# One adaLN transformer block on one core: out projections by single tiles in every even step, and an ffn product in plain fp32

## The reference

```
h = layernorm(x) * (1 + ca) + sa
x = x + ga * attention(h) @ Wo.T          # 8 heads of 64, keys and values from a latent of 64
h = layernorm(x) * (1 + cb) + sb
x = x + gb * (h @ weight.T + pooled(h) @ disha)
```

## Time and profile before

| | |
|---|---|
| three runs, median (lowest to highest) | 3177.59 us (3172.59 to 3179.52) |
| the profiled execution | 3168.62 us |
| its span, first to last instruction | 3166.8 us |
| mean granted TensorE clock | 0.997 |
| busy: PE / DVE / ACT / POOL | 96% / 71% / 54% / 80% |
| attention slot 8 of 16, step 0 to step 0 | 192.80 us |

### The profile page before, as it was taken

The page is one execution under the profiler, slowest core; times in us unless marked ns, Lnnn a source line. Parts: engine busy times, 40 slices in busy tenths (PEclk is TensorE's granted clock), DMA queues, the critical chain, the costliest instruction groups (busy, mean ns, idle before and its releaser), DMA issues.

```text
span 3166.8 us, 45191 instructions
## 1 busy us (share of the span) xinstructions
PE 3047.3 (96%) x15394; PEld 1679.0 (53%) x15394; DVE 2236.2 (71%) x2484; ACT 1721.5 (54%) x3209; POOL 2549.1 (80%) x1520
## 2 busy tenths in 40 slices
PE   6999999999999999999999999999999999999998
PEld 4445555555555555555555455555555555555445
DVE  5567767776777777777767777776777777776665
ACT  3555555555555555555555555555555555555544
POOL 3878787988878888788887878888787887888787
PEclk9999999999999999999999999999999999999999
DMA  2111111121112111121111211211121111211111
GB/s 83 43 43 51 53 57 44 48 64 45 54 45 68 41 48 58 48 61 45 51 48 51 64 44 48 64 45 51 48 67 42 48 58 48 61 38 45 48 45 47
DMA packets 165348, 162.92 MB, mean 51 GB/s; under 512 B 62208, under 2 KB 113536, under 8 KB 165120
## 3 DMA queue, kind: packets, MB, share of 16 engines
q1 hardware_dynamic: 165120, 160.05, 17.2%
HBM read 74.40 MB, written 17.33 MB: 29 GB/s over the span
## 4 chain that ended last, share of the span: by engine, by line
PE 61%; DVE 16%; POOL 10%; issue 6%; ACT 6%; DMA 1%; SPq 0%; DVEq 0%; POOLq 0%; ACTq 0%
PE ps_mix L628 17%; PE ps_score L649 11%; PE ps_score L651 9%; POOL prob_sum L1021 8%; PE ps_max L677 7%; DVE neg_max L1173 6%; PE ps_side L614 6%; PE ps_side L743 4%; PE ps_side L762 3%; ACT probs L851 2%; DVE query L1215 2%; PE ps_side L729 2%; ACT query L897 2%; DVE mixed_lo L1191 1%; DVE h_lo L1205 1%
## 5 line engine op out<-in xcount | busy, mean ns | idle before, releaser
L1021 POOL TENSOR_TENSOR prob_sum<-prob_sum,probs 128x1024 f32<-128x1024 f32 x768 | 1898.6, 2472 | 329.6 <-ACT probs L851 255.7
L1173 DVE TENSOR_REDUCE neg_max<-ps_max 128x1 f32<-128x1024 f32 x1024 | 1202.9, 1216 | 391.2 <-PE ps_max L677 387.2
L851 ACT ACTIVATE probs<-ps_score 128x512 f32<-128x512 f32 x2048 | 1112.3, 596 | 559.6 <-PE ps_score L651 506.6
L628 PE MATMUL ps_mix<-probs,values 128*64 128x512 f32 x4096 | 937.1, 599 | 0.8 <-ACT probs L851 0.8
L649 PE MATMUL ps_score<-query,key_hi 128*128 128x512 f32 x2048 | 888.9, 434 | 31.6 <-ACT probs L851 25.1
L651 PE MATMUL ps_score<-query_m,key_lo 128*128 128x512 f32 x2048 | 809.5, 395 | 0.0
L628 PEld LDWEIGHTS ps_mix<-probs,values 128*64 128x64 f32 x4096 | 271.7, 137 | 534.1 <-issue 532.9
L649 PEld LDWEIGHTS ps_score<-query,key_hi 128*128 128x128 f32 x2048 | 384.4, 188 | 316.9 <-ACT probs L851 156.1
L1021 POOL TENSOR_TENSOR prob_sum<-probs 128x1024 f32<-128x1024 f32 x128 | 317.4, 2479 | 142.1 <-ACT probs L851 142.1
L651 PEld LDWEIGHTS ps_score<-query_m,key_lo 128*128 128x128 f32 x2048 | 386.7, 189 | 42.5
L677 PE MATMUL ps_max<-key_hi,query 64*128 64x512 f32 x2048 | 375.7, 444 | 27.5 <-DVE neg_max L1173 26.1
(11 more groups left out here) (191 smaller groups left out, 2759.3 us busy)
## 6 DMA issues: line engine op xcount, KB each, us to landing
query_m<-query SPq DMA_DIRECT2D x128, 256.0 KB, 2.4
query_m<-query SPq DMA_DIRECT2D x256, 128.0 KB, 2.4
recip<-recip_scratch SPq DMA_DIRECT2D x254, 128.0 KB, 2.9
x_in<-in_L_attn_x_dram SPq DMA_DIRECT2D x32, 512.0 KB, 4.7
x_mid<-in_L_attn_x_dram SPq DMA_DIRECT2D x64, 256.0 KB, 4.2
out_dram<-x_mid SPq DMA_DIRECT2D x64, 256.0 KB, 2.2
denoms<-recip SPq DMA_DIRECT2D x508, 1.0 KB, 1.7
gates<-gates_scratch SPq DMA_DIRECT2D x16, 256.0 KB, 4.5
```

Source lines behind the costliest of these rows:

```text
L628: last = nc.tensor.matmul(ps_mix[j * R:j * R + R, :], values[par][:, k, :], probs[:, (STEPS * z.c + s) % RING, j * HALF:(j + 1) * HALF], s ...
L851: nc.scalar.activation(probs[:, (STEPS * z.c + s) % RING, half * HALF:(half + 1) * HALF], ps_score[half], ACT.Exp, scale=SCALE).then_inc(e ...
L1021: nc.gpsimd.tensor_tensor(out=total[:, :], in0=before, in1=probs[:, now % RING, :], op=ALU.add).then_inc(adds_done, 1)
L1173: nc.vector.tensor_reduce(neg_max[:, col:col + 1], ps_max[j][:, :], AX_X, ALU.max, negate=True).then_inc(maxima_done, 1)
```

## The change

1. `out_proj` goes by single token tiles: eight pieces of 12 matmuls in place of four of 24, each with its own sum and statistics on DVE. They stand in steps 2, 6, 10, 14, 22, 26, 34, 38. Before, the four stood in 10, 14, 22, 30.
2. The plan's other pieces are moved so that each of the 32 even steps has exactly one. Before, steps 2, 6, 58 and 60 had none.
3. The ffn multiplies `h2_t` and the gated weights as they are, in fp32: 4 matmuls a chunk in place of 12. `h2_hi`, `h2_lo`, `w_ffn_hi`, `w_ffn_lo` and their instructions are gone; `h2_t` has two buffers, and the gated weights a buffer of their own (before they lay in `x_norm2`, for which the norm waited).
4. The statistics for the second half of the next batch's norm are taken in steps 55 to 61 of the slot before, and `apply` stands in steps 57 and 1 in place of 43 and 2.
5. SP loads the first chunk of x for the next slot's out projection in step 40, the others in step 1 as before.

```diff
-AHEAD_LOAD, AHEAD_STATS, AHEAD_APPLY = 22, (29, 33, 37, 41), 43
-NEXT_LOAD, NEXT_STATS, NEXT_APPLY = 47, (1, 1, 1, 1), 2
+AHEAD_LOAD, AHEAD_STATS, AHEAD_APPLY = 22, (29, 33, 37, 41), 57
+NEXT_LOAD, NEXT_STATS, NEXT_APPLY = 47, (55, 57, 59, 61), 1
...
 PLAN = {
-    "query": (32, 36, 40, 44, 48, 52, STEPS, STEPS + 4),
+    "query": (32, 40, 44, 52, 56, 60, STEPS, STEPS + 4),
     "norm_t": (8, 12, 16, 20),
     "latent": (24, 28),
     "values_t": (42, 46),
...
-    "out_proj": (10, 14, 22, 30),
-    "norm2": (11, 27, 36, 51),
-    "norm2_t": (18, 34, 50, 56),
-    "h2_split": (21, 37, 53, 57),
-    "ffn": (26, 38, 54, 62),
+    "out_proj": (2, 6, 10, 14, 22, 26, 34, 38),
+    "norm2": (9, 27, 41, 50),
+    "norm2_t": (18, 36, 48, 58),
+    "ffn": (30, 50, 54, 62),
 }
...
                     elif kind == "ffn":
-                        need(pe, h2_split, CHUNKS * b + i + 1)
+                        drained(pe, z, "norm2_t", i)
                         if i == 0:
-                            need(pe, w_ffn_split, NF * (b + 1))
+                            pe.wait_ge(ffn_gated, b + 1)
                         need(pe, side_drained[room], count)
-                        whole, hi, lo = h2_parts(z, i)
-                        products = [(hp, wp, f) for f in range(NF)
-                                    for hp, wp in ((hi, w_ffn_hi), (lo, w_ffn_hi), (hi, w_ffn_lo))]
                         for j in range(CT):
-                            for q, (hp, wp, f) in enumerate(products):
-                                last = nc.tensor.matmul(side[:, j * D:(j + 1) * D], hp[:, f, j * P:(j + 1) * P],
-                                                        wp[:, f, :], start=(q == 0), stop=(q == len(products) - 1))
+                            for f in range(NF):
+                                last = nc.tensor.matmul(side[:, j * D:(j + 1) * D], h2_t[i % 2][:, f, j * P:(j + 1) * P],
+                                                        w_ffn_gated[:, f, :], start=(f == 0), stop=(f == NF - 1))
...
-                            nc.vector.tensor_tensor(x_mid[i][:, :, :], side.rearrange("p (j d) -> p j d", j=CT),
-                                                    x_mid[i][:, :, :], ALU.add).then_inc(side_drained[room], 1)
+                            nc.vector.tensor_tensor(x_mid[g][:, j, :], side[:, 0:D], x_mid[g][:, j, :], ALU.add).then_inc(side_drained[room], 1)
```

More of the change, by code:

```diff
@@ L316, in adaln_block @@
         gates = sb("gates", [P, 2, D])
[L317 to L321, removed]
+        h2_t = [sb(f"h2_t{i}", [P, NF, CT * P]) for i in range(2)]
         stage = [probs[:, 2:, :].rearrange("p a t -> p (a t)"), mixed[:, :, :].rearrange("p a t -> p (a t)")]
@@ L824, in _ @@
             nc.scalar.activation(s_silu[:, 0, :, :], s_c, ACT.Exp, scale=-1.0).then_inc(exp_c_made, 1)
-            def split_h2(z, g):
-                drained(act, z, "norm2_t", g)
-                old = g - 1 if z.has_c else g - 2
-                if old >= 0:
-                    full(act, z, "ffn", old)
-                else:
-                    last_full(act, z)
-                whole, hi, lo = h2_parts(z, g)
-                nc.scalar.activation(hi, whole, ACT.Copy).then_inc(h2_hi_done, 1)
             act.wait_ge(fold_a_kept, 6)
@@ L858, in slot @@
                         if z.has_o:
-                            full(act, z, "out_proj", CHUNKS - 1)
+                            full(act, z, "out_proj", NT - 1)
                         nc.scalar.activation(w_out_hi[:, :, :], w_out_gated[:, :, :], ACT.Copy).then_inc(w_out_hi_done, 1)
-                    for g in range(CHUNKS):
-                        if z.has_o and z.has_c and s == z.step("h2_split", g):
-                            split_h2(z, g)
                     for g in range(CHUNKS):
@@ L1192, in slot @@
                                                     hi.bitcast(F32), ALU.subtract).then_inc(mixed_split, 1)
+                    if z.n == 1 and s in (1, 3):
+                        for i in range(NT // 2):
+                            statistics(z.n, s // 2, i)
                     for i, t in enumerate(NEXT_STATS):
-                        if z.n == 1 and s == t:
-                            statistics(z.n, 0, i)
-                        if z.has_n and not first(z) and s == (t + 2 if z.n == 1 else t):
-                            statistics(z.n, 1, i)
+                        if z.has_nn and not first(z) and s == t:
+                            statistics(z.n + 1, 1, i)
                     for i, t in enumerate(AHEAD_STATS):
@@ L1200, in slot @@
                             statistics(z.n + 1, 0, i)
-                    for g in range(CHUNKS):
-                        if z.has_o and s == z.step("h2_split", g):
-                            need(dve, h2_hi_done, CHUNKS * z.o + g + 1)
-                            whole, hi, lo = h2_parts(z, g)
-                            nc.vector.tensor_tensor(lo, whole, hi.bitcast(F32), ALU.subtract).then_inc(h2_split, 1)
                     for kind, i, b, w in z.at(s):
```

84 lines of the change are left out of this document (34 added, 50 removed).

## The result

The changed kernel takes 3087.20 us (median of 4 runs, 3085.94 to 3087.66) against 3178.56 for the kernel before on the same chip (4 runs, 3172.59 to 3181.75): a ratio of 0.9714, with an interval of 0.9697 to 0.9731. On a second occasion it was 3088.84 against 3172.77, 0.9729 (0.9716 to 0.9742).

A forecast was written before the change was run, and what follows sets the result against it. PE, busy 96%, bounds the kernel, with waits inside its steps. A slot: -2.4 + 1.8 - 3.5 = -4.1 us, 14 times -57, slot 15 -3, last slot -2: -62, median 3115.6 us, range 3090 to 3155.

The forecast's parts named there:

- the waits that go: PE's waits in eleven steps of a slot: 1.3 of 4.8 us remain, so -3.5 us a slot.
- the price of fp32: Ffn chunks on PE: fp32 costs 0.39 to 0.60 us more each, taken as 0.45, so +1.8 us a slot.
- the step from the profiled execution to the median: Whole kernel: the median lies 9 us above the profiled execution, making 3107 into 3115.6 us.
- slot 15: The slot that prepares no next batch and has longer waits of its own: -3 us.
- What bounds, and tiles in every even step: PE's steps in a slot: eight of 2.44 us replace four of 3.85 and four empty ones, -2.4 us a slot.
- step 58 would be at 2.44: Sign of being right: steps 2, 6, 58 and 60 at 2.44 us, odd steps behind them at 1.68.
- What I had feared as next late: Reductions before short steps 8, 16, 48, up to 1.1 us each; `w_out_lo` before 48, up to 1.1; transposes 0.1 each.
- The reason that I gave for the waits: DVE loses 7.9 us of split work a slot and gains 1.4, so reductions and drains PE awaits come sooner.
- The last slot and the gaps on POOL and SP: Last slot -2 us; `apply` in step 57 and SP's x load cost nothing as long as the gaps hold.
- (a): Rival: fp32 ffn weight loads lie bare, a chunk takes 3.5 us, slot +2.1, kernel 3209 us; chance 0.06.
- (b): Rival: the waits only move, all 4.8 us return elsewhere, -0.6 us a slot, kernel 3167 us; chance 0.13.
- (c): Rival: all waits go, fp32 as cheap as L628, -5.3 us a slot, 3098 us; within the forecast's 0.80.

The follow-up runs named there:

- g: Kernel b with the first ffn split moved from step 21 to 27 and the weights' low parts to step 25: 3070.36 us, ratio 0.9671 to the kernel before.
- Experiment e: Changed kernel with out projection by chunks again, 24 matmuls in each of steps 6, 14, 26, 38: 3139.71 us, ratio 0.9891 to the kernel before.
- f: Changed kernel with 12 unsplit fp32r matmuls per ffn chunk instead of 4 fp32, result three times too large: 3065.91 us, ratio 0.9657 to the kernel before.
- b: Changed kernel with the old fp32r ffn, split in steps 21, 37, 51, 60: 3098.43 us, ratio 0.9774 to the kernel before.
- c: Changed kernel plus the old split's ACT copies and DVE subtractions as dead work nobody reads: 3143.28 us, ratio 0.9921 to the kernel before.
- h: Kernel before with only `mixed_hi` and `mixed_lo` of chunk 1 moved from step 13 to 12: 3152.53 us against 3169.24, ratio 0.9946.
- a: Kernel before with only the fp32 ffn, `h2_t` in two buffers and a buffer for gated weights: 3151.93 us against 3171.60, ratio 0.9942.
- d: Changed kernel with the next norm at its old steps, statistics in 1, apply in 43 and 2: 3094.33 us, ratio 0.9760 to the kernel before.

## Why the prediction was right in direction and too small

Four sizes erred to the same side, and together they put the time outside the range: the waits that go (3.5 us a slot, measured 4.1, so 8 us in all), the price of fp32 (0.45 a chunk, measured 0.30, 8 us), the step from the profiled execution to the median (9, measured 1.3, 8 us) and slot 15 (3, measured 8.7, 6 us). The mechanism failed in one place: I put what part 3 brings down to work that DVE loses, and g shows that it is where this work stood.

**What bounds, and tiles in every even step.** Right. Experiment e measures the bare geometry at 2.3 us a slot where the sum had 2.4. One detail was wrong without touching the sum: I wrote that step 58 would be at 2.44, but the plan puts four transposes there, and it stays at 1.49; it is step 34 that gained a tile.

**The price of fp32.** The first term of the sum that was mis-sized. I took 0.45 a chunk from the rows of L772 and gave 0.39 to 0.60 as bounds; the runs show 0.30 (steps 30 and 31) and 0.31 (f), below the lower bound. Eight records 0.216 apart are 1.73 us against 1.40. The row that I read had it: eight records of L772 take 1.90, and one lasts 0.38, so they start (1.90 - 0.38) / 7 = 0.217 apart; I took the way to L677 into the price. The lower bound came from L628, whose 0.224 for 256 columns carries the group's ends: inside it pairs of records start 0.43 apart (0.215 for 256 columns), but 0.48 behind the first pair and 0.53 from the last one to the next work. The ffn steps took 2.55 and not 2.8 to 3.0, since part of the price shows in the step behind, where I hadn't looked for it. That is 0.15 x 4 x 14 = 8 us.

**The waits.** Right in kind, too careful in size. I let 1.3 us of 4.8 remain; the steps of the changed kernel, laid against the bare lengths (188.0 - 2.4 + 1.2 = 186.8), leave 0.5. What I had feared as next late didn't come: the short steps 8, 16 and 48 take 1.48, 1.50 and 1.51, where I had allowed 1.1 more for each, and `w_out_lo` ahead of step 48 costs nothing. A tile's sum takes 0.41 us and the next reduction stands 1.1 behind the sum's start (1630.33 to 1631.41 in slot 8, against 1.94 for a chunk in the earlier trace rows), so the chain that made step 25 wait is short enough even with the multiplication ahead of it. What remains lies in steps 17, 20, 23 and 60, 0.08 to 0.14 each, and 0.06 in step 47. Slot 8, from which I took the 4.8, is 0.15 us longer than the mean of the 14 slots, so 4.1 of 4.65 us went. That is 0.6 x 14 = 8 us.

**The reason that I gave for the waits** holds only in part. I credited them to work that DVE loses, and the work is not what counts: g does all of it and has no such wait, f does none and is no shorter. Part 3 removed a badly placed split, and a better place for it does as well. On the new plan fp32 is a loss of 18 us against g.

**Slot 15.** Sized loosely at -3, measured -8.7. Maxima and products of its step 25, before and after:

```profile
3022.74 0.73 PE L677 MATMUL ps_max<-key_hi,query 64*128 64x512 f32 x4 [2.11 <-DVE neg_max L1173]
3023.40 5.35 PE L628 MATMUL ps_mix<-probs,values 128*64 128x512 f32 x16
```

```profile
2944.21 0.73 PE L665 MATMUL ps_max<-key_hi,query 64*128 64x512 f32 x4
2944.88 3.65 PE L616 MATMUL ps_mix<-probs,values 128*64 128x512 f32 x16
```

And the granted clock (the number ahead of the last two) while these products ran, before and after:

```profile
3024.00:3027.00 3.00, 3.00 (x10) 0.78 (x8) 3.00 (x4) 0.00 (x0) 0.00 (x0) 0.50 0.00 0
```

```profile
2944.00:2949.00 5.00, 5.00 (x30) 1.51 (x28) 2.41 (x3) 1.40 (x3) 3.82 (x2) 1.00 0.03 8
```

Step 25 of this slot takes 9.84 us before and 5.97 after: 2.11 of wait ahead of the maxima, and products that take 5.35 where they need 3.65. The second part is TensorE's clock: it is at the lower of its two levels (1.2 GHz) from 3024 to 3027, a microsecond after the wait ended, and the products inside that stretch last 1.06 us each in place of 0.59. So 1.7 of the 3.9 us that the step lost were lost clock, a term that no part of my sum had. Kernels b, c and h have such a stretch in this step too, behind waits of 2.65, 2.64 and 2.10; in a, where 0.49 of the wait is left, the products take 3.65 again. The steps without projections are short in this slot (step 24 takes 1.48, not 2.76), so PE comes to the maxima earlier while DVE's list ahead of the reduction is the same, with a `w_ffn_lo` of 1.70 us, a split of 2.89 and the multiplication of 2.88. What DVE loses there PE no longer waits for, and I had priced this with the waits of a full slot. Step 41 takes 7.25 and 6.22.

**The last slot and the gaps on POOL and SP.** -2.7 against -2, and no new wait. Before, there was a stretch from 3154 to 3157 at a granted clock of 0.50, in which the matmuls of an ffn chunk start 0.21 apart and not 0.12; the changed kernel has none in this slot, so an unknown part of the -2.7 is clock too. `apply` in 57 and 1 is worth some 5 to 7 us (d) with no cost.

**From the profiled execution to the median.** The sum gave 3168.6 - 62 = 3107, and I added 9 us, the distance of the kernel before. The changed kernel's profiled execution is 3085.94, 1.3 under its median. Of the miss of 28 us, 21 belong to the sum and 8 to this step. The distance belongs to the one execution, not to the kernel. The 21 are 17 in the slots 1 to 14 (5.3 us a slot against 4.1), 6 in slot 15 and 1 at the end, less 3 that were lost ahead of slot 1.

**The rivals.** (a), bare weight loads, is ruled out: a chunk's 8 records would have taken 3.5 us and take 8 x 0.216 = 1.73. (b), waits that only move, is ruled out for tiles by the changed kernel itself, and for one step by h; c shows that it is real where the moved work is behind the multiplication. (c) is what happened in the slots: -5.3 us, as its sum had, but by luck: 0.4 more of the waits is left than it had, and fp32 is 0.4 cheaper. It had 3098 because of the 9 us and slot 15. I had put it at the lower side of a range that ended 8 us below it; slot 15 (6) and the median's distance (8), less the 3 lost ahead of slot 1, used up 11.

## What to carry to other kernels

When PE waits for a small drain on another engine, first read what stands ahead of that drain in the engine's list, and try another step for it before replacing the algorithm: one split moved by one step was worth 17 us here (h), and one split and the weights' low parts moved to other steps were worth 28 (g), while the fp32 product that made the work unnecessary cost 23 us on PE. Side work goes best in pieces just long enough to cover the wait of the step that it stands in; a piece twice as long beside an empty step paid 51 us for the same matmuls. And a price per chunk is to be read from the distance between records inside a group, without the entry, and checked in the step behind as well. Where a wait is long, read the granted clock behind it before the wait alone is priced: in slot 15 the low clock cost 1.7 us behind a wait of 2.1.

## What the runs showed of the hardware

**A DVE operation with two SBUF inputs has no fixed length beside POOL.** The subtraction of 128x512 took 2.88 us in b and 0.68 in g. POOL at these moments, in b and in g (start, length, engine, operation):

```profile
1624.21 13.01 POOL L1031 TENSOR_TENSOR prob_sum<-prob_sum,probs 128x1024 f32<-128x1024 f32 x5
```

```profile
1636.02 1.61 POOL L1085 TENSOR_SCALAR x_norm<-x_mid,rstd 128x256 f32<-128x256 f32 x2 [0.18 <-POOL rstd L989]
```

In b POOL is in a row of five additions of 2.4 to 2.65 us, and the subtraction takes about one of them longer; in g POOL is at the norm, which reads one tensor. So it is in whole traces. In the kernel before, 30 subtractions of this shape stood in additions for over 90% of their length and took 2.71 in the median, up to 2.90; the four that met no addition took 0.66 to 0.69. In g 17 met none, 16 of them beside the norm, and took 0.66 to 0.69. `mixed_lo` in h is of this kind: the 31 that met no addition took 1.21 to 1.27. Operations with an input from PSUM keep their length through all of it (the sum of a tile, L1256, takes 0.41 to 0.43 in b, all 128 of them). The Trainium skill has this in "SBUF — State Buffer", section "SBUF: two separate sides": DVE's operations with two SBUF inputs and GpSimd's contend for a pair of ports that is held for a whole instruction while the other side is blocked. The trace agrees in size, 2.88 - 0.68 = 2.2 us for an addition of 2.4. It does not agree for the norm: in g POOL runs an instruction that reads SBUF in those moments and no delay shows. No run here stopped POOL, so the cause rests on the rows' agreement and was not tried by itself.

**Full fp32 weight loads lie under fp32 matmuls.** The loads of L747 take all 128 rows and 190 ns each, and the records they belong to follow each other each 0.216 us. By the rule of "TensorE: Matmul & The Clock Gate", Part 3, in the Trainium skill, that a load overlaps only for another group of rows, a chunk would take an estimated 8 x (0.216 + 0.190) = 3.2 us; it takes 1.73, so the trace disagrees for fp32 as it did for fp32r.

**Behind a long wait TensorE's clock was low.** In step 25 of slot 15 PE sat idle 2.11 us, and from 3024 to 3027 the granted clock was 0.50; the products took 5.28 us up to the next work, and 3.58 in the changed kernel, at 1.00 throughout. No run tried this by itself.

**An fp32 group is paid in part behind itself.** The first fp32r record behind it (L637 at 1653.88) lasts 0.58 us, while the one behind the twelve fp32r matmuls of a tile (L637 at 1585.11) lasts 0.40.
